# A masked attention kernel on TensorE: the four transposes of a step stand between its three score matmuls

## What is computed

```python
q = x @ Wq.T + bq
k = x @ Wk.T + bk
v = x @ Wv.T + bv
scores = q @ k.T / jnp.sqrt(jnp.asarray(d, q.dtype))
scores = jnp.where(adj > 0, scores, neg)
attention = jax.nn.softmax(scores, axis=-1)
att = attention @ v
x = _layernorm(x + jax.nn.elu(att), axis=-1)
```

## Time and profile before

| | before |
|---|---|
| device time, median of 3 runs | 509.17 us (508.66 to 509.61) |
| the profiled execution: span, first to last instruction | 508.1 us |
| PE busy | 485.9 us, 96% of the span |
| PEld busy | 365.9 us, 72% |
| DVE busy | 408.9 us, 80% |
| ACT busy | 362.8 us, 71% |
| POOL busy | 166.4 us, 33% |
| TensorE's mean granted clock | 0.994 of 2.4 GHz |

### The profile page before, as it was taken

How to read it: one execution, slowest core, us unless ns; L and a number is a source line. 1 busy time by engine, 2 the same in 40 slices (tenths; PEclk the granted TensorE clock), 3 DMA queues, 4 the chain that set the end, 5 groups by cost and what they waited for, 6 DMA issues and landing times.

```text
span 508.1 us, 12547 instructions
## 1 busy us (share of the span) xinstructions
PE 485.9 (96%) x3971; PEld 365.9 (72%) x3971; DVE 408.9 (80%) x720; ACT 362.8 (71%) x682; POOL 166.4 (33%) x372
## 2 busy tenths in 40 slices
PE   5998999999999999999999999999999999999991
PEld 3665777777777777777777777777777777777871
DVE  0859888888898888888888888888988888889750
ACT  3776677778677767777667677777677677776783
POOL 0150133333333233333232333332333333333225
PEclk9999999999999999999999999999999999999997
DMA  8635454445545454545454545455454544450000
GB/s 250 268 124 158 147 158 146 151 135 162 158 143 161 138 160 140 148 151 161 137 165 139 157 141 152 140 164 149 150 154 145 150 149 142 153 163 13 6 6 11
DMA packets 28074, 71.70 MB, mean 141 GB/s; under 512 B 2976, under 2 KB 11680, under 8 KB 28064
## 3 DMA queue, kind: packets, MB, share of 16 engines
q1 hardware_dynamic: 27632, 71.51, 45.8%
q10 hardware_dynamic: 432, 0.07, 0.1%
HBM read 69.47 MB, written 2.10 MB: 141 GB/s over the span
## 4 chain that ended last, share of the span: by engine, by line
PE 35%; ACT 20%; issue 16%; DVE 13%; POOL 12%; DMA 1%; ACTq 1%; DVEq 1%; POOLq 0%; SPq 0%
PE ps_t L557 10%; DVE scores L431 7%; PE ps_out L573 6%; ACT scores L329 6%; POOL expm L252 5%; ACT p_hi L337 5%; DVE p_lo L442 4%; PE ps_scores L545 3%; PE ps_scores L544 3%; PE ps_scores L543 3%; PE ps_out L575 3%; POOL y L255 3%; ACT att L342 3%; ACT act_junk L358 3%; POOL res L250 2%
## 5 line engine op out<-in xcount | busy, mean ns | idle before, releaser
L442 DVE SCALAR_TENSOR_TENSOR p_lo<-ps_t,p_hi 128x512 f16<-128x512 f32 x256 | 173.5, 688 | 67.2 <-ACT p_hi L337 62.5
L337 ACT ACTIVATE p_hi<-ps_t 128x512 f16<-128x512 f32 x256 | 151.3, 594 | 100.6 <-PE ps_t L557 92.5
L573 PE MATMUL ps_out<-v_parts,p_hi 128*128 128x257 f16 x1024 | 199.3, 274 | 0.7 <-DVE p_lo L442 0.7
L575 PE MATMUL ps_out<-v_parts,p_lo 128*128 128x129 f16 x1024 | 185.8, 218 | 0.0
L557 PEld LDWEIGHTS ps_t<-ident,scores 128*128 128x128 f32 x1024 | 122.3, 141 | 65.5 <-DVE p_lo L442 21.4
L557 PE MATMUL ps_t<-ident,scores 128*128 128x128 f32 x1024 | 156.2, 275 | 5.2 <-DVE p_lo L442 1.4
L431 DVE CUSTOM_DVE_ANT_0 scores<-ps_scores,adj 128x1024 f32<-128x1024 f32 x128 | 155.6, 1216 | 0.1
L329 ACT ACTIVATE scores<-scores,neg_max 128x1024 f32<-128x1024 f32 x128 | 146.2, 1142 | 0.0
L573 PEld LDWEIGHTS ps_out<-v_parts,p_hi 128*128 128x128 f16 x1024 | 99.1, 97 | 11.7 <-DVE p_lo L442 1.0
L575 PEld LDWEIGHTS ps_out<-v_parts,p_lo 128*128 128x128 f16 x1024 | 100.6, 98 | 2.9
L543 PE MATMUL ps_scores<-k_hi,q_hi 128*128 128x512 f16 x256 | 96.7, 378 | 0.7 <-DVE max_parts L431 0.7
(11 more groups left out here) (49 smaller groups left out, 269.2 us busy)
## 6 DMA issues: line engine op xcount, KB each, us to landing
adj<-in_adj_dram SPq DMA_DIRECT2D x128, 512.0 KB, 4.1
x_rows<-in_x_dram SPq DMA_DIRECT2D x4, 512.0 KB, 6.2
out_dram<-y_out SPq DMA_DIRECT2D x32, 64.0 KB, 1.6
w_rows<-in_L_gnn_Wk_dram SPq DMA_DIRECT2D x1, 64.0 KB, 4.3
bv_rows<-in_L_gnn_bv_dram ACTq DMA_DIRECT2D x1, 64.0 KB, 4.4
w_rows<-in_L_gnn_Wq_dram SPq DMA_DIRECT2D x1, 64.0 KB, 4.1
w_rows<-in_L_gnn_Wv_dram SPq DMA_DIRECT2D x1, 64.0 KB, 4.3
b_cols<-in_L_gnn_bq_dram ACTq DMA_DIRECT2D x1, 0.5 KB, 2.9
```

Source lines behind the costliest of these rows:

```text
L337: nc.scalar.activation(p_hi[:, g % PSLOTS, :], ps_t[g % 2][:, :], ACT.Copy, scale=P_SCALE).then_inc(phi_ready, 1)
L442: nc.vector.scalar_tensor_tensor(out=p_lo[:, g % PSLOTS, :], in0=ps_t[g % 2][:, :], scalar=P_SCALE, in1=p_hi[:, g % PSLOTS, :], op0=ALU.mu ...
L573: nc.tensor.matmul(ps_out[s][:, 0:2 * D + 1], p_hi[:, g % PSLOTS, blk], v_parts[:, k, 0:2 * D + 1], start=(k == 0), stop=False)
L575: last = nc.tensor.matmul(ps_out[s][:, D:2 * D + 1], p_lo[:, g % PSLOTS, blk], v_parts[:, k, D:2 * D + 1], start=False, stop=(k == TILES - 1))
```

## The change

Inside the steady loop a new function `scores_between_transposes` issues a step's score matmuls and its transposes in the order S1, T0, S2, T1, S3, T2, T3. Both waits of the transposes stand directly ahead of T0, so they are now behind S1 and ahead of S2 and S3. `scores_ready` is still signalled by S3 and `pt_ready` by T3. The values follow as before. Outside the loop (the first two periods and the last two) nothing changes, and no other engine's program changes.

```diff
+            def scores_between_transposes(i, j, ti, ts, g):
+                c = j // 2
+                place = ps_scores[c % 2][:, j % 2 * BANK:(j % 2 + 1) * BANK]
+                cols = slice(j * BANK, (j + 1) * BANK)
+                rows = bass.ds(i * P, P)
+                def turn(b):
+                    k = g * BLOCKS + b
+                    return nc.tensor.transpose(ps_t[g % 2][:, b * P:(b + 1) * P], s_sb[ts][:, k * P:(k + 1) * P], ident[:, :])
+                if j % 2 == 0:
+                    pe.wait_ge(masked_ready, PIECES * i + c - 1)
+                nc.tensor.matmul(place, q_hi[:, rows], k_hi[:, cols], start=True, stop=False)
+                pe.wait_ge(exp_done, PIECES * ti + g // 2 + 1)
+                pe.wait_ge(plo_ready, STEPS * ti + g - 1)
+                turn(0)
+                nc.tensor.matmul(place, q_hi[:, rows], k_lo[:, cols], start=False, stop=False)
+                turn(1)
+                last = nc.tensor.matmul(place, q_lo[:, rows], k_hi[:, cols], start=False, stop=True)
+                if j % 2 == 1:
+                    last.then_inc(scores_ready, 1)
+                turn(2)
+                turn(3).then_inc(pt_ready, 1)
...
                 for j in range(STEPS):
-                    if has_scores:
+                    g = (j - LAG_T) % STEPS
+                    mixed = warm and has_scores and has_last and has_first
+                    if mixed and j < LAG_T - STEPS:
+                        scores_between_transposes(i, j, i - 2, s, g)
+                    elif mixed:
+                        scores_between_transposes(i, j, i - 1, 1 - s, g)
+                    elif has_scores:
                         scores(i, j, not warm and s == 0)
...
-                    if j < LAG_T - STEPS and has_last:
+                    if j < LAG_T - STEPS and has_last and not mixed:
                         transposes(i - 2, s, g, False)
-                    if j >= LAG_T - STEPS and has_first:
+                    if j >= LAG_T - STEPS and has_first and not mixed:
                         transposes(i - 1, 1 - s, g, not warm)
```

More of the change, by code:

```diff
@@ L589, in period @@
                             project(n)
-                    g = (j - LAG_T) % STEPS
-                    if j < LAG_T - STEPS and has_last:
+                    if j < LAG_T - STEPS and has_last and not mixed:
                         transposes(i - 2, s, g, False)
-                    if j >= LAG_T - STEPS and has_first:
+                    if j >= LAG_T - STEPS and has_first and not mixed:
                         transposes(i - 1, 1 - s, g, not warm)
```

## The result

| | before | after |
|---|---|---|
| device time, median of 4 runs | 509.23 us (508.66 to 509.61) | 524.87 us (523.84 to 525.02) |
| ratio | | 1.0292, 95% interval 1.0262 to 1.0322 |
| span of the profiled execution | 508.1 us | 523.0 us (its own time: 524.72 us) |

The kernel became 2.9% slower, by 15.6 us. The forecast was 10.8 us slower (520.0 us), so the direction was right and the time lies inside the stated range of 515.4 to 526.2. It lies outside the forecast's own range of 518.4 to 521.7, and some 5 us are unaccounted for so far.

The account below looks back on a forecast made before the run. A closed loop of 14.41 us a tile, not PE's 14.05, was taken as the bound. 28 tiles cost 10.5 us, tile 31 0.3: 10.8 us slower, 520.0 us; own range 518.4 to 521.7, whole range 515.4 to 526.2.

Parts of the forecast that it names:

- rival C: At step 5, a later DVE mask makes T0 wait inside the loop: 6.2 us more, 526.2 us; chance 0.13.
- A transpose holds the array for 0.11 us by itself: In every mixed step on PE: transposes keep 0.11 us whatever load follows, so the order itself costs zero.
- Rival A: At T0 and T1 of each step: hidden weight loads make transposes faster, 0.11 us a step, 509.0 us; chance 0.07.
- The loop through step 3: Closed chain of waits over PE, ACT, POOL and DVE, 14.41 us a tile; S2 and S3 add 0.43 us.
- Rival B: Step 3's wait is timed by ACT, POOL and DVE alone; S2 and S3 paid once, 509.6 us; chance 0.04.
- The new stall at step 1: T0 waits 0.31 us for ACT's exponential; costs nothing in 28 tiles, 0.3 us in tile 31.
- The margin of 0.19 us at step 5: DVE's low part allows T0 at 275.40, PE wants it at 275.59, so DVE's delay stays hidden.
- T1's 0.06 us of lateness: Behind the waiting T0 of step 3: should go with S2 there instead, leaving 0.375 us a tile.
- S3's later signal at odd steps: `scores_ready` comes 0.22 us later, more at step 3, delaying DVE's mask work; taken as hidden, no cost.

Follow-up runs that it names:

- step 3 alone: The changed kernel with the mixed order restricted to step 3, all other steps in the old order: 521.51 us, ratio 1.0238.

## Why the prediction was right, and where it missed

The direction and the main mechanism held. That the time lies in the stated range at all is in part luck: it is 3.2 us above the forecast's own range, in the room that was given to rival C, and C did not happen where it was placed.

- *A transpose holds the array for 0.11 us by itself.* S2 and S3 follow a transpose by 0.11 us in the changed kernel, and the two orders take equal time without a binding loop (500.34 and 500.22). Rival A is out. The Trainium skill ("TensorE: Matmul & The Clock Gate", section "Wait — 56ns, not 53.3ns?") gives 56 ns from start to start for matmuls of 128 columns, measured with bf16. The trace agrees for the float16 value matmuls of 129 columns (L581: 0.056 us to the next start), and not for these float32 transposes: 0.109 us in every undisturbed row, whether the next weight load is long or short.
- *The loop through step 3 becomes longer by S2 and S3.* Forecast 0.43 us a tile for this term, measured 0.433 with step 3 alone. Rival B (loop not closed through PE) is out: it would have paid this once.
- *The new stall at step 1 costs nothing in the 28 tiles.* Held, but by less than I thought: it is a loop of its own, of 14.60 us, which is hidden only as long as the first is longer. I had called it a stall that is swallowed; I had not seen that it closes through PE as well. Its size was off too: 0.48 us instead of 0.31. Of this 0.09 is expm's, and 0.08 is that T0 starts 0.13 us behind the exponential's end, where I took the 0.05 that it has behind DVE's low part. In tile 31 it cost 0.33 us, forecast 0.3. And because this stall comes first, PE's idle time at step 3 is 0.26 to 0.29 us, not the 0.72 that I said the profile would show.
- *The margin of 0.19 us at step 5.* It held: PE does not wait there in the 28 tiles (only in tile 30 is T0's successor late, by 0.06). Rival C, as placed, did not happen.

Two terms of the sum were mis-sized, and together they are 4.1 of the missing 4.9 us.

- *"T1's 0.06 us of lateness should go, because S2 and not T1 follows T0."* It did not. S2 follows a T0 that had to wait by 0.165 us (264.42 to 264.59), exactly as T1 did. I had charged the lateness to T1's long float32 load. The short float16 load of S2 doesn't take it away: what counts is T0's own load, which waits too and so has no lead. Wherever in the ten traces the matmul behind T0 is more than 0.01 us late, it starts 0.166 to 0.171 us after the start of T0's load, also where T0 itself is on time (249.74 to 249.91). 28 x 0.056 = 1.6 us. I had this as the upper end of the forecast's own range.
- *S3's later signal at odd steps was called hidden.* I followed it on DVE only, to the low part of step 5. It went another way: at step 7 it moves DVE's mask piece, this holds up POOL's expm by 0.1 us, and expm lies in the loop that I had written out from the chain of waits. 28 x 0.091 = 2.5 us. This was rival C's idea (a DVE delay enters the loop) with the wrong place and the wrong price.

The sum again with the measured terms: 28 tiles x 0.53 = 14.9 us (0.522 in the settled ones; a few at the two ends differ by up to 0.12), tile 2 0.1 and tile 31 0.3, together 15.3 us, against 15.6 between the medians. From the first S1 to the end the two profiled executions differ by 15.29 us (488.06 and 503.35), so the sum is complete for this part. The last 0.3 us are within what the start of the kernel varies by.

## What to carry to other kernels

Where a wait of a hand-ordered engine ends last only once in a while, work that stands ahead of it is free and work behind it is not: do not move a wait forward past work that could run in its shadow. Write out the loop that such a wait closes, engine by engine; its length against the busiest engine's own work (here 14.42 against 14.05 us) says both what an edit costs and what another could gain. Here the gain was on DVE, which was busy 80%: moving one independent instruction of it out of the loop brought 1.8% with the old order of TensorE. With the mixed order, which closes the second loop too, two had to move to come to the same time (514.83 us with one, 500.34 with two).

## What the runs showed of the hardware

- POOL's 128x128 `tensor_tensor` (expm, two inputs in SBUF) takes 0.40 us alone. Where it starts while DVE's `tensor_scalar` on 128x1024 runs, it ends 0.25 to 0.26 us behind the end of that one, in every tile of the eight kernels in which the two overlap, whether it started 0.17 us after the mask or 0.02, and so lasts 0.77 to 0.93 us. Beside DVE's masked piece, whose one input is in PSUM, it keeps its 0.40 us. The Trainium skill ("SBUF — State Buffer", section "SBUF: two separate sides") describes an exclusive lock on a port pair that DVE and GpSimd share, held for a whole instruction; the direction agrees, and the rows add that POOL's instruction ends 0.25 us after the other one, less than the 0.40 us that it takes alone.
- The matmul behind a transpose whose float32 weight load had to wait starts 0.166 to 0.171 us after the start of that load, with a float32 load behind it as with a float16 one. If the load runs ahead of its transpose by 0.06 us or more, nothing is lost and the distance between the two matmuls is 0.109 us; if it starts with it, 0.165.
- T0 starts 0.06 us behind the end of DVE's instruction that releases it, and 0.13 us behind the end of ACT's.
